# A scan layer and an attention layer in one kernel: block the scan on TensorE, move small operations to GpSimd, reorder all engines

## The chip, the cores and the metric
The kernel runs on one core of a Trainium2 chip, as one launch. The metric is the device time of that launch in microseconds (us); smaller is better. The core has TensorE (PE, matmuls; its weight loads are listed as PEld), VectorE (DVE), ScalarE (ACT), GpSimd (POOL) and SyncE (SP), which here only issues DMAs. Each engine works through its own instructions in order, and they wait for one another by semaphores.

## The reference
The input x is 128 sequences of 64 tokens of 256 channels, fp32, and cond is 128 x 512. Two layers are added to x one after the other:

```
xr, gate = split(x @ W_in.T); xr += cond; xc = silu(causal conv, 4 taps, of xr)
xn = layernorm(xc) * g + b                       # 512 channels
Bm, Cm, dt = split(xn @ W_xproj.T, 3)            # 16 states each
dt = tanh(dt @ W_dt.T + b_dt) * 0.01;  Ad = 1 + dt * (-tanh(A_log));  Bd = Bm * min(norm(xn), 1)
h = clip(h * Ad + Bd x xn, -10, 10); y_t = C_t . h       # 64 steps in order, h: 16 x 512
x = x + (y + D * xn) * silu(gate) @ W_out.T
# second layer: x * style, layernorm, q, k, v by 256 x 256 weights scaled per sequence,
# softmax attention of 16 heads over the 64 tokens, output projection, and a skip projection of v
x = x + attention(x, styles = cond)
```

## The kernel before
**Tiles and chains.** A tile is two sequences, 128 tokens: 64 tiles. The scan works on chains of 8 sequences (4 tiles): 8 sequences x 16 states fill the 128 partitions, 16 chains in all. Even chains run in lane r = 0, odd ones in lane r = 1, half a chain apart, so that both lanes are live most of the time. One step of the program advances each lane by a slice of 8 scan steps.

**Three parts.** Part A makes xn and B, C, dt of a tile; xn goes to DRAM in three bf16 parts (`a_parts`, `xn_parts`), whose sum is nearly the fp32 value, and D * xn too (`a_dx`). Part B is the scan. `prepare` turns dt of a chain into a running product `pr` and its reciprocal `rp`, so that the scan becomes an addition with clipping. On TensorE, `spread` makes the increment of one scan step in one lane: one bf16 matmul of 64 rows into `ps_u` [128, 512]. On VectorE, `scan_step` adds it to the state with bounds `hi` and `lo` (one custom instruction, L1429) into a ring `gc` of four. On TensorE, `read_out(u)` contracts two states in both lanes with the spread-out C (`cms`) into `ps_y`, 32 columns for each of four column groups. ScalarE copies `ps_y` to `y_sb`, SyncE stores it. Part C loads a tile's y (`c_y`) and D * xn (`c_dx`), adds them (`c_sum_skip`), multiplies by the silu of the gate (`c_gate_product`), projects out (`c_project_out`), adds the residual (`c_residual`, `c_x1`), and then does the attention layer.

**The order of the work** is written out by hand: each engine has a function `step(i)` with one long list of pieces, called for i = 0, 1, ... A piece's argument says how many steps behind it runs: `a_transpose_x(i)` works on tile i, `a_stats(i - 2)` on tile i - 2, scan slices on `sig = i - SCAN_LAG`, part C on `c0 = i - C_LAG` and below. There are 88 steps. Three PSUM banks (`bank[0..2]`) are passed around; `taken(...)` names the reader that must be done with a bank before the next matmul writes it. So each wait is either for data or for a buffer, and what stands ahead of a waiting piece on its engine doesn't matter, only what stands behind it.

**Pieces named below.** On SyncE: `store_parts`, `store_out`, `store_dx`, `load_wu`, `load_s1`, `load_xs` (six DMAs, 1 MB, the operand of the next slice), `store_y` (four DMAs), `load_y` (c_dx, then c_y, the latter behind the stores of the whole chain), `load_x`, `load_cx`, `store_bct`; and once per chain `load_raw`, `store_b`, `load_w` (the weights of the spread). On GpSimd: `a_half`, `a_sum` (the sum of the four taps), `a_var`, `a_root`, `a_bias`, `a_gain`, `a_shift` (xn), `a_skip`, `a_first_rest` and `a_second_rest` (the second and third bf16 part), `c_style`, `c_join`, `c_final`. On VectorE besides the scan: `a_silu`, `a_stats`, `a_mean_var`, `a_take_bc`, `a_scale_b`, `a_offset`, `spread_c`, `c_silu`, `c_max`, `c_subtract` and others. In the profile, L797 is `spread`, L813 `read_out`, L741 `a_transpose_x`, L823 `c_transpose_x`, L780 `a_transpose_bc`, L881 `c_project_k`, L1390 `a_scale_b`, L1440 `spread_c`, L1461 `c_gate_product`, L525 `a_half`, L591 `a_second_rest`, L651 `c_join`, L541 `a_var`.

## Time and profile before
| | |
|---|---|
| median of 3 runs | 2017.59 us (2012.55 to 2017.72) |
| the profiled execution | 2018.07 us, span 2016.3 us |
| mean granted TensorE clock | 0.917 of full speed |
| TensorE busy | 1736.2 us (86%), 12460 matmuls |
| TensorE weight loads | 1108.4 us (55%), beside the matmuls |
| VectorE busy | 1552.4 us (77%), 2754 instructions |
| ScalarE busy | 1161.7 us (58%) |
| GpSimd busy | 1024.1 us (51%), 1360 instructions |
| DMA moved | 224.25 MB, mean 111 GB/s |

The span runs from the first to the last instruction of the profiled execution; the execution's own time is a little longer. Busy is time in which the engine works on at least one instruction, as a sum over the span. The pipeline fills and drains, so a share of the whole span is a mean over very different stretches: TensorE is busy for half of the first tenth and for nearly all of the middle. The granted clock is in parts of full speed (1.0 is 2.4 GHz, 0.5 is 1.2 GHz). A matmul of fp32 data appears as two instructions. A row of the order of time may merge several instructions of a group; what stands in brackets is the idle time ahead of it and what ended that.

### The profile page before, as it was taken

To read this page: it belongs to the slowest core of one execution; us is meant where nothing else is said; L and a number is where in the kernel's file an instruction comes from. 1 tells how busy PE (TensorE), PEld (TensorE's weight loads), DVE (VectorE), ACT (ScalarE), POOL (GpSimd) and SP (SyncE) were. 2 spreads that over 40 slices of the span, in tenths; PEclk is the share of its full clock that TensorE was granted. 3 is DMA by queue.
4 is the path that set the end of the run, shared out by engine and by line. 5 is a ranking of instruction groups with operands and counts; after the bars stand their busy time and mean duration, and the time that the engine had idled before them with its cause. 6 is when DMAs were issued, how large, how long until landed. Compare 5 with 4: busy or idle time off the path is not lost. (4 is left out here: it accounts for less than half of the span.)

```text
span 2016.3 us, 41197 instructions
## 1 busy us (share of the span) xinstructions
PE 1736.2 (86%) x12460; PEld 1108.4 (55%) x12460; DVE 1552.4 (77%) x2754; ACT 1161.7 (58%) x2921; POOL 1024.1 (51%) x1360
## 2 busy tenths in 40 slices
PE   5337677889999999999999999999999989999775
PEld 4224333446666656666656666656665555555564
DVE  1515588889999999999999999989998888754332
ACT  4455554466676767676767676767676434344433
POOL 1576655566566656565666665656564521111220
PEclk8556788899999999999999999999999999999888
DMA  3013344555554555555554555555555554431200
GB/s 94 30 51 82 87 115 115 131 138 134 125 135 131 133 129 135 134 135 136 133 130 125 124 135 128 133 125 132 133 135 130 128 118 107 103 87 56 66 29 20
DMA packets 222713, 224.25 MB, mean 111 GB/s; under 512 B 54240, under 2 KB 179552, under 8 KB 222496
## 3 DMA queue, kind: packets, MB, share of 16 engines
q1 hardware_dynamic: 222496, 221.62, 44.3%
q8 instruction: 104, 1.70, 0.4%
q14 instruction: 113, 0.93, 0.2%
HBM read 150.36 MB, written 71.17 MB: 110 GB/s over the span
## 5 line engine op out<-in xcount | busy, mean ns | idle before, releaser
L1429 DVE CUSTOM_DVE_ANT_0 gc<-ps_u,gc,hi 128x512 f32<-128x512 f32 x1008 | 781.5, 799 | 109.8 <-PE ps_u L797 90.9
L813 PE MATMUL ps_y<-gc,cms 128*32 128x512 f32 x2048 | 309.2, 641 | 0.8 <-DVE cms L1440 0.7
L797 PE MATMUL ps_u<-xs_sb,stage 64*128 64x512 bf16 x1024 | 256.9, 467 | 28.8 <-DVE gc L1429 25.3
L1084 ACT ACTIVATE a_tap<-a_xr,conv_w 128x128 f32<-128x128 f32 x768 | 244.4, 395 | 9.4 <-DVE a_xr L1334 9.0
L797 PEld LDWEIGHTS ps_u<-xs_sb,stage 64*128 64x128 bf16 x1024 | 92.2, 167 | 282.7 <-issue 174.4
L541 POOL TENSOR_TENSOR a_ve<-a_mv,eps 128x1 f32<-128x1 f32 x64 | 12.1, 189 | 446.8 <-DVE a_mv L1361 446.8
L751 PE MATMUL ps<-a_xT,WinT 128*128 128x128 f32 x1024 | 157.9, 318 | 76.7 <-ACT a_z L1101 72.2
L751 PEld LDWEIGHTS ps<-a_xT,WinT 128*128 128x128 f32 x1024 | 145.0, 226 | 107.9 <-issue 102.5
L525 POOL TENSOR_TENSOR a_tap<-a_tap 128x512 f32<-128x512 f32 x128 | 159.7, 1269 | 58.0 <-ACT a_tap L1084 58.0
L1227 ACT ACTIVATE c_e<-c_s 128x512 f32<-128x512 f32 x128 | 80.6, 630 | 176.5 <-DVE c_s L1519 175.0
L1205 ACT ACTIVATE c_kbd<-ps,mask 128x256 f32<-128x256 f32 x256 | 100.3, 474 | 102.3 <-PE ps L881 102.3
L651 POOL TENSOR_TENSOR c_f<-c_f 128x256 f32<-128x256 f32 x64 | 46.8, 731 | 206.1 <-DVE c_f L1544 205.9
L850 PE MATMUL ps<-WoutT,c_ygT 128*128 128x256 f32 x512 | 138.1, 419 | 0.5 <-ACT c_xT L1155 0.5
L832 PE MATMUL ps<-WinT,c_xT 128*128 128x512 f32 x256 | 131.1, 635 | 0.0
L870 PE MATMUL ps<-c_zT,L1T 128*128 128x128 f32 x1024 | 125.0, 275 | 2.1 <-DVE c_sg L1452 2.1
L870 PEld LDWEIGHTS ps<-c_zT,L1T 128*128 128x128 f32 x1024 | 121.0, 192 | 3.7 <-issue 2.7
L599 POOL TENSOR_TENSOR a_nrm<-a_ss,half_pow 128x1 f32<-128x1 f32 x64 | 50.6, 791 | 140.6 <-ACT a_xg L1117 140.6
L850 PEld LDWEIGHTS ps<-WoutT,c_ygT 128*128 128x128 f32 x512 | 104.8, 216 | 15.5 <-issue 1.3
L622 POOL TENSOR_TENSOR c_xm<-c_x,c_s 128x256 f32<-128x256 f32 x64 | 47.9, 748 | 127.2 <-DVE c_x L1468 120.3
L1334 DVE TENSOR_TENSOR a_xr<-ps,condT 128x512 f32<-128x512 f32 x64 | 43.7, 682 | 82.0 <-PE ps L751 76.3
L1084 ACT ACTIVATE a_tap<-a_xr,conv_b,conv_w 128x128 f32<-128x128 f32 x256 | 105.1, 487 | 0.0
L881 PE MATMUL ps<-c_zT,L1T 128*128 128x128 f32 x512 | 84.4, 315 | 20.5 <-DVE a_bc L1382 20.5
(165 smaller groups left out, 3709.4 us busy)
## 6 DMA issues: line engine op xcount, KB each, us to landing
xs_sb<-xn_parts SPq DMA_DIRECT2D x256, 192.0 KB
xn_parts<-a_parts SPq DMA_DIRECT2D x128, 192.0 KB, 3.2
skip_d_xn<-a_dx SPq DMA_DIRECT2D x64, 256.0 KB, 8.0
xs_sb<-xn_parts SPq DMA_DIRECT2D x128, 128.0 KB
scan_out<-y_sb SPq DMA_DIRECT2D x256, 64.0 KB
c_dx<-skip_d_xn SPq DMA_DIRECT2D x64, 256.0 KB, 3.7
c_y<-scan_out SPq DMA_DIRECT2D x64, 256.0 KB, 4.8
c_wu<-style_rows SPq DMA_DIRECT2D x128, 128.0 KB, 3.0
```

The lines of the kernel that those rows point to most:

```text
L525: pool.tensor_tensor(first, first, second, ALU.add).then_inc(s[f"a_half{h}"], 1)
L751: mm = pe.matmul(ps[:, m * TOK:(m + 1) * TOK], WinT[:, k, m * P:(m + 1) * P], a_xT[:, k, :], start=(k == 0), stop=(k == KC - 1))
L797: pe.matmul(ps_u[r][t % 2][:, :], weights[:, :, l * STEPS + t], xs_sb[rows, l % 2, t, :], start=True, stop=True).then_inc(s[f"b_u{r}"], 1)
L813: pe.matmul(ps_y[quad:quad + 32, :], cms[:, v, r, 32 * u:32 * (u + 1)], gc[r][:, (2 * u + v) % RING, :], start=(u == 0), stop=(u == UNITS ...
L832: mm = pe.matmul(ps[:, :], c_xT[:, k, :], WinT[:, k, DI:2 * DI], start=(k == 0), stop=(k == KC - 1))
L850: mm = pe.matmul(ps[:, 0:DM], c_ygT[:, m, :], WoutT[:, m, :], start=(m == 0), stop=(m == MC - 1))
L870: mm = pe.matmul(ps[:, (o + c) * TOK:(o + c + 1) * TOK], L1T[:, w, k, c * P:(c + 1) * P], c_zT[:, k, :], start=(k == 0), stop=(k == KC - 1))
L881: mm = pe.matmul(ps[:, c * TOK:(c + 1) * TOK], L1T[:, 1, k, c * P:(c + 1) * P], c_zT[:, k, :], start=(k == 0), stop=(k == KC - 1))
L1084: ins = act.activation(a_tap[:, tap, m, :].rearrange("p (r t) -> p r t", r=2), a_xr[:, m, :, tap:tap + S], ACT.Identity, bias=bias, scale= ...
L1205: ins = act.activation(c_kbd[:, h, :, :].rearrange("p k t -> p (k t)"), ps[:, 0:KC * TOK], ACT.Copy, scale=mask4[:, h:h + 1])
L1227: act.activation(c_e[:, g, :], c_s[:, g, :, :].rearrange("p h t -> p (h t)"), ACT.Exp)\
L1429: dve._custom_dve(bass.dve_ops.TENSOR_ADD_SAT, out=gc[r][:, t % RING, :], in0=ps_u[r][t % 2][:, :], in1=before, s0=hi[:, c % 4, col:col + ...
```

## The change
The arithmetic stays the same except for the form of a few small operations. What changes:

1. **Scan block.** `spread(2k)`, `spread(2k + 1)` and a readout stand together on TensorE as `scan_block(sig, k)`, four times a step; the readout is that of the block before (`read_out(k - 1)`, and for k = 0 the last one of the slice before). Before, the eight spreads and four readouts stood apart among the other work.
2. **VectorE to GpSimd.** `a_offset` (as a product and a sum), `a_scale_b`, `spread_c`, `c_gate_product`, and all of the preparation of a chain but the first three operations (`split_b`, 8 operations in place of 8). `cms` gets a second buffer.
3. **New order** of the lists of all five engines, with shorter lags: `SCAN_LAG` 8 for 9, `C_LAG` 16 for 17, part C from c0 to c0 - 4 in place of c0 to c0 - 6; 84 steps in place of 88.

```diff
@@ constants
-    SCAN_LAG = 9
-    C_LAG = 17
-    STEP_COUNT = TILES + C_LAG + 7
+    SCAN_LAG = 8
+    C_LAG = 16
+    STEP_COUNT = TILES + C_LAG + 4
@@ TensorE
+            def scan_block(sig, k):
+
+                spread(sig, 2 * k)
+                spread(sig, 2 * k + 1)
+                if k > 0:
+                    read_out(sig, k - 1)
+                else:
+                    read_out(sig - 1, UNITS - 1)
@@ GpSimd, moved here from VectorE
+            def spread_c(sig):
+                for r in range(2):
+                    if chain_of(sig, r):
+                        c, l = chain_of(sig, r)
+                        pool.wait_ge(s["b_prep"], PREP * (c + 1))
+                        pool.wait_ge(s[f"b_read{r}"], 8 * (HEAD + slice_no(c, l) - 1))
+                        pool.tensor_tensor(
...
+            def c_gate_product(n):
+                if not on(n):
+                    return
+                pool.wait_ge(s["c_sg"], at(n))
+                pool.wait_ge(s["c_yd"], at(n))
+                pool.wait_ge(s["c_ygTp"], at(n - 1))
+                pool.tensor_tensor(c_yg[:, :], c_yd[:, :], c_sg[:, :], ALU.mult).then_inc(s["c_yg"], 1)
...
@@ SyncE's step
+                store_parts(i - 4)
+                store_out(c0 - 4)
+                store_dx(i - 3)
+                load_wu(c0 - 3)
+                load_s1(c0)
+                load_xs(sig + 1, 0)
+                load_xs(sig + 1, 1)
                 store_y(sig - 1)
+                load_y(c0)
                 load_x(i + 1)
+                if chain_due(i, 1) is not None:
+                    store_b(chain_due(i, 1))
+                    load_w(chain_due(i, 1))
+                load_cx(c0 + 1)
+                store_bct(i - 3)
                 if chain_due(i, 2) is not None:
                     load_raw(chain_due(i, 2))
@@ GpSimd's step, as it is now
+                if chain_due(i, 1) is not None:
+                    split_b(chain_due(i, 1))
+                spread_c(sig)
+                a_var(i - 2)
+                a_root(i - 2)
+                a_bias(i - 2)
+                a_scale_b(i - 3)
+                a_half(i - 1, 0)
                 c_sum_skip(c0)
+                c_gate_product(c0)
...
+                a_sum(i - 1)
+                a_second_rest(i - 3)
+                c_style(c0)
+                a_first_rest(i - 2)
+                c_var(c0)
+                c_root(c0)
                 a_norm_root(i - 2)
```

On TensorE, in a steady step, around the readout at the step's border; before (L797 is `spread`, L813 `read_out`; L823, L892 and L918 transpose, L850 is `c_project_out`):

```order
L813 MATMUL ps_y<-gc,cms 32x512 x4
L797 MATMUL ps_u_0<-xs_sb,stage 128x512 x2
L823 MATMUL ps<-ident,c_x 128x128 x2
L892 MATMUL ps<-ident,c_vd 128x128 x4
L797 MATMUL ps_u_1<-xs_sb,stage 128x512 x2
L918 MATMUL ps<-ident,c_e 128x128 x4
L850 MATMUL ps<-WoutT,c_ygT 128x256 x4
L918 MATMUL ps<-ident,c_e 128x128 x4
L797 MATMUL ps_u_0<-xs_sb,stage 128x512 x2
```

And after, the scan block k = 2 and the next one (L868 is `spread`, L884 `read_out`, L922 transposes yg, L989 are the scores, L931 is `c_project_out`):

```order
L868 MATMUL ps_u_0<-xs_sb,stage 128x512 x2
L868 MATMUL ps_u_1<-xs_sb,stage 128x512 x2
L884 MATMUL ps_y<-gc,cms 32x512 x4
L922 MATMUL ps<-ident,c_yg 128x128 x4
L989 MATMUL ps<-c_kbd,c_q 64x256 x8
L931 MATMUL ps<-WoutT,c_ygT 128x256 x4
L868 MATMUL ps_u_0<-xs_sb,stage 128x512 x2
L868 MATMUL ps_u_1<-xs_sb,stage 128x512 x2
L884 MATMUL ps_y<-gc,cms 32x512 x4
```

Two pairs of spreads and a readout now stand together, with three or four other pieces between two blocks.

On SyncE, from `store_bct` on, an ordinary step before:

```order
L340 DMA b_c_dt<-a_bcT 48x2x64
L455 DMA out_dram<-c_out 128x256
L411 DMA scan_out<-y_sb 8x4x512 x4
L447 DMA c_wu<-style_rows 64x512 x2
L332 DMA a_x<-in_x_dram 128x256
L351 DMA xn_parts<-a_parts 192x1x512 x2
L420 DMA c_dx<-skip_d_xn 128x512
L422 DMA c_y<-scan_out 128x512
L400 DMA xs_sb<-xn_parts 24x8x512 x2
L400 DMA xs_sb<-xn_parts 16x8x512
L400 DMA xs_sb<-xn_parts 24x8x512 x2
L400 DMA xs_sb<-xn_parts 16x8x512
```

And after, from `store_parts` on:

```order
L353 DMA xn_parts<-a_parts 192x1x512 x2
L457 DMA out_dram<-c_out 128x256
L360 DMA skip_d_xn<-a_dx 128x512
L449 DMA c_wu<-style_rows 64x512 x2
L440 DMA c_s<-style_rows 64x256 x2
L402 DMA xs_sb<-xn_parts 24x8x512 x2
L402 DMA xs_sb<-xn_parts 16x8x512
L402 DMA xs_sb<-xn_parts 24x8x512 x2
L402 DMA xs_sb<-xn_parts 16x8x512
L413 DMA scan_out<-y_sb 8x4x512 x4
L422 DMA c_dx<-skip_d_xn 128x512
L424 DMA c_y<-scan_out 128x512
```

The load of c_y stood ahead of the six loads of xs and behind one group of stores of y; it now stands behind both.

On GpSimd, from `c_sum_skip` (the row of c_yd) on, before:

```order
L614 TENSOR_TENSOR c_yd<-c_dx,c_y 128x512
L576 TENSOR_TENSOR a_xn<-a_xg,b_row 128x512
L599 TENSOR_TENSOR a_nrm<-a_ss,half_pow 128x1
L622 TENSOR_TENSOR c_xm<-c_x,c_s 128x256
L606 TENSOR_TENSOR a_dx<-a_xn,d_row 128x512
L584 TENSOR_TENSOR a_r<-a_xn,a_parts 128x512
L541 TENSOR_TENSOR a_ve<-a_mv,eps 128x1
L542 TENSOR_TENSOR a_nmu<-a_mv,neg_one 128x1
L550 TENSOR_TENSOR a_rs<-a_ve,half_pow 128x1
L558 TENSOR_TENSOR a_nb<-a_rs,a_nmu 128x1
```

And after, from the row behind `c_sum_skip`, the gate product, to `a_second_rest`:

```order
L679 TENSOR_TENSOR c_yg<-c_yd,c_sg 128x512
L716 TENSOR_TENSOR c_f<-c_f 128x256
L569 TENSOR_TENSOR a_xg<-a_z,g_row 128x512
L709 TENSOR_TENSOR c_nb<-c_rs,c_nmu 128x1
L579 TENSOR_TENSOR a_xn<-a_xg,b_row 128x512
L663 TENSOR_TENSOR a_dx<-a_xn,d_row 128x512
L528 TENSOR_TENSOR a_tap<-a_tap 128x512
L723 TENSOR_TENSOR c_out<-c_f,c_x 128x256
L611 TENSOR_TENSOR a_base<-g_proj,a_nb 128x48
L614 TENSOR_TENSOR a_base<-a_base,b_proj 128x48
L536 TENSOR_TENSOR a_cv<-a_tap 128x512
L594 TENSOR_TENSOR a_parts<-a_r,a_parts 128x512
```

The sum of c_y and c_dx was followed by operations on tiles whose gate product came a step later on VectorE; now the gate product of the same tile is the next row, and the row of a_parts comes last of the twelve.

## Rows read from the trace of the kernel before
**Rows 1.** Stretches: length, busy us of PE, PEld, DVE, ACT, POOL; clock, DMA
```profile
527.50:1516.70 989.20, 955.52 (x7335) 613.59 (x7336) 912.48 (x1620) 670.86 (x1711) 601.41 (x798) 0.98 0.53 132
1516.70:1852.60 335.90, 306.81 (x2203) 186.37 (x2203) 255.86 (x452) 144.42 (x335) 95.38 (x152) 0.95 0.44 105
1852.60:2016.00 163.40, 116.35 (x912) 94.22 (x912) 50.81 (x102) 63.60 (x148) 29.20 (x52) 0.86 0.14 43
```

**Rows 2.** TensorE on a_x (whole run, then 527 to 1517) and c_x
```profile
L741 PE MATMUL ps<-ident,a_x x128: 272/292/476, 29.3 to 1516.8; 128*128 128x128 f32 x128
L741 PE MATMUL ps<-ident,a_x x78: 272/283/303, 527.5 to 1516.8; 128*128 128x128 f32 x78
L823 PE MATMUL ps<-ident,c_x x128: 272/300/473, 332.1 to 1910.4; 128*128 128x128 f32 x128
```

**Rows 3.** TensorE in order of time, an ordinary step (start, length)
```profile
1067.01 0.30 PE L780 MATMUL ps<-ident,a_bc 128*128 128x128 f32 x1 [0.35 <-DVE c_s L1519]
1067.24 1.07 PE L813 MATMUL ps_y<-gc,cms 128*32 128x512 f32 x8
1068.24 0.47 PE L797 MATMUL ps_u<-xs_sb,stage 64*128 64x512 bf16 x2
1068.63 0.44 PE L823 MATMUL ps<-ident,c_x 128*128 128x128 f32 x2
```

**Rows 4.** The same, a step in which a chain is prepared
```profile
1023.65 2.04 PE L881 MATMUL ps<-c_zT,L1T 128*128 128x128 f32 x8 [1.96 <-DVE a_bc L1382]
...
1025.63 1.94 PE L813 MATMUL ps_y<-gc,cms 128*32 128x512 f32 x8
```

**Rows 5.** VectorE's groups by line (busy us, mean ns, idle before and releaser)
```profile
L1429 DVE CUSTOM_DVE_ANT_0 gc<-ps_u,gc,hi 128x512 f32<-128x512 f32 x1008 | 781.5, 799 | 109.8 <-PE ps_u L797 90.9 <-PE ps_y L813 0.4
...
L1440 DVE TENSOR_TENSOR cms<-cp,mask 128x64 f32<-128x64 f32 x128 | 75.9, 653 | 0.0
...
L1461 DVE TENSOR_TENSOR c_yg<-c_yd,c_sg 128x512 f32<-128x512 f32 x64 | 47.5, 742 | 0.0
```

**Rows 6.** The scaling of B on VectorE, 527 to 1517 (ns min/median/max)
```profile
L1390 DVE TENSOR_SCALAR a_bc<-a_bc,a_nrm x38: 224/1160/1171, 542.8 to 1506.8; 128x16 f32<-128x16 f32 x38
```

**Rows 7.** SyncE in order of time, an ordinary step (start, length)
```profile
1069.21 2.78 SPq L411 DMA_DIRECT2D scan_out<-y_sb  x4
1072.10 1.14 SPq L447 DMA_DIRECT2D c_wu<-style_rows  x2
1073.97 1.23 SPq L351 DMA_DIRECT2D xn_parts<-a_parts  x2
1075.29 0.56 SPq L420 DMA_DIRECT2D c_dx<-skip_d_xn  x1
1075.89 0.44 SPq L422 DMA_DIRECT2D c_y<-scan_out  x1
1076.38 2.71 SPq L400 DMA_DIRECT2D xs_sb<-xn_parts  x6
1079.13 0.68 SPq L358 DMA_DIRECT2D skip_d_xn<-a_dx  x1
1079.86 1.14 SPq L438 DMA_DIRECT2D c_s<-style_rows  x2
```

**Rows 8.** Landing of the loads of c_y, 527 to 1517
```profile
DMA to landing us min/median/max: 2.9/4.8/7.6
```

**Rows 9.** Landing of the loads of c_x, 527 to 1517
```profile
DMA to landing us min/median/max: 4.1/6.9/8.7
```

**Rows 10.** GpSimd in order of time (start, length)
```profile
1064.26 2.49 POOL L525 TENSOR_TENSOR a_tap<-a_tap 128x512 f32<-128x512 f32 x2
...
1066.70 1.15 POOL L591 TENSOR_TENSOR a_parts<-a_r,a_parts 128x512 bf16<-128x512 f32 x1
...
1087.91 0.73 POOL L651 TENSOR_TENSOR c_f<-c_f 128x256 f32<-128x256 f32 x1
```

**Rows 11.** GpSimd's longest wait, 527 to 1516 (us in total, times, longest)
```profile
POOL a_ve L541 <- DVE a_mv L1361: 303.1, 38, 12.4
```

More of the change, by code:

```diff
@@ L103, in mamba_attention_kernel @@
         eps = sb("eps", [P, 2])
+        bounds = sb("bounds", [P, 2])
         zeros = sb("zeros", [P, DI])
@@ L241, in mamba_attention_kernel @@
         head_start = {
-            "dve": """a_xr:1 a_xc:1 a_bnd:1 a_mv:1 a_nm:1 a_base:1 a_bc:1 a_bs:1 b_g0:1 b_g1:1 b_cms0:1 b_cms1:1
-                c_sg:1 c_yg:1 c_x1:1 c_st1:1 c_mv:1 c_q:1 c_vs:1 c_mx0:1 c_mx1:1 c_sub0:1 c_sub1:1 c_rc:1 c_o:1 c_f:1""",
+            "dve": """a_xr:1 a_xc:1 a_bnd:1 a_mv:1 a_nm:1 a_bc:1 b_g0:1 b_g1:1
+                c_sg:1 c_x1:1 c_st1:1 c_mv:1 c_q:1 c_vs:1 c_mx0:1 c_mx1:1 c_sub0:1 c_sub1:1 c_rc:1 c_o:1 c_f:1""",
             "pe": """a_xTp:1 a_inp:1 a_xcT:1 a_proj:1 a_bcTp:1 b_u0:8 b_u1:8 b_read0:8 b_read1:8 c_xTp:1 c_gate:1 c_ygTp:1
@@ L502, in _ @@
             pool.memset(neg_one[:, :], -1.0)
+            pool.memset(bounds[:, 0:1], CLIP)
+            pool.memset(bounds[:, 1:2], -CLIP)
             pool.memset(a_bc[:, :], 0.0).then_inc(s["w_bc"], 1)
@@ new lines, in a_scale_b, with split_b @@
+            def a_scale_b(n):
+                if not on(n):
+                    return
+                pool.wait_ge(s["a_bc"], at(n))
+                pool.wait_ge(s["a_nm"], at(n))
+                pool.tensor_tensor(a_bc[:, 0:DS], a_bc[:, 0:DS], a_nrm[:, 1:2].to_broadcast([P, DS]), ALU.mult)\
+                    .then_inc(s["a_bs"], 1)
+            def split_b(c):
+                k, done = c % 4, PREP * c
+                pool.wait_ge(s["b_pr"], 3 * (c + 1))
+                if c > 0:
+                    pool.wait_ge(s["b_bst"], 48 * c)
+                if c >= 4:
+                    pool.wait_ge(s[f"b_g{c % 2}"], HEAD + STEPS * slice_no(c - 4, SLICES))
+                pool.tensor_tensor(bd[:, :], raw[:, 0, :], rp[:, :], ALU.mult).then_inc(s["b_prep"], 1)
+                pool.tensor_tensor(b_parts[:, 0, :], raw[:, 0, :], rp[:, :], ALU.mult).then_inc(s["b_prep"], 1)
+                pool.tensor_tensor(cp[:, k, :], raw[:, 1, :], pr[:, :], ALU.mult).then_inc(s["b_prep"], 1)
+                pool.wait_ge(s["b_prep"], done + 2)
+                pool.tensor_tensor(bd[:, :], bd[:, :], b_parts[:, 0, :], ALU.subtract).then_inc(s["b_prep"], 1)
+                pool.tensor_tensor(hi[:, k, :], rp[:, :], bounds[:, 0:1].to_broadcast([P, S]), ALU.mult).then_inc(s["b_prep"], 1)
+                pool.wait_ge(s["b_prep"], done + 4)
+                pool.tensor_tensor(b_parts[:, 1, :], bd[:, :], zeros[:, 0:S], ALU.add).then_inc(s["b_prep"], 1)
+                pool.tensor_tensor(lo[:, k, :], rp[:, :], bounds[:, 1:2].to_broadcast([P, S]), ALU.mult).then_inc(s["b_prep"], 1)
+                pool.wait_ge(s["b_prep"], done + 6)
+                pool.tensor_tensor(b_parts[:, 2, :], bd[:, :], b_parts[:, 1, :], ALU.subtract).then_inc(s["b_prep"], 1)
@@ L1029, in _ @@
+                c_transpose_p(c0 - 2, 0, bank[0],
+                              taken(("c_sub0", c0 - 2), ("c_vs", c0 - 2), ("c_sg", c0), ("c_xT", c0),
+                                    ("a_bc", i - 3)))
             for i in range(STEP_COUNT):
@@ L1453, in c_silu @@
                     .then_inc(s["c_sg"], 1)
-            def c_gate_product(n):
-                if not on(n):
-                    return
-                dve.wait_ge(s["c_sg"], at(n))
-                dve.wait_ge(s["c_yd"], at(n))
-                dve.wait_ge(s["c_ygTp"], at(n - 1))
-                dve.tensor_tensor(c_yg[:, :], c_yd[:, :], c_sg[:, :], ALU.mult).then_inc(s["c_yg"], 1)
             def c_residual(n, ps):
```

331 lines of the change are left out of this document (136 added, 195 removed).

## The prediction
> **What bounds the kernel now.** I read the split of the span into stretches first, then the times at which a step begins, then the order of time on TensorE, on SyncE's queue and on GpSimd. The run has three stretches. From 527.5 to 1516.7 us all three parts work (input part A, scan, output part C) and TensorE is busy 955.5 of 989.2 us at a granted clock of 0.98, VectorE 912.5, ScalarE 670.9, GpSimd 601.4 [rows 1]. The transposition that opens a step of A runs 78 times there, two per step, so 38 steps lie between the first and the last: 989.2 / 38 = 26.0 us a step [rows 2]. Then 13 steps with scan and C in 336 us, and the rest of C in 163 us at a clock of 0.86 [rows 1].
>
> In an ordinary step TensorE waits for almost nothing: the one wait seen is 0.35 us, before the transposition of a_bc [rows 3]. In every fourth step, where VectorE prepares the coefficients of a chain, it waits 1.96 us and then runs at half speed for a while: the readout takes 1.94 where it takes 1.07 otherwise [rows 3, 4]. So the steady stretch is bound by TensorE, with VectorE (24.0 us busy a step) close behind. GpSimd is idle about 8 us a step waiting for a_mv alone (303 us in 38 waits) [rows 11].
>
> **TensorE's work.** Eight pairs of scan matmuls stand alone now, and each costs 0.39 us from its start to the next operation's start (1068.24 to 1068.63) [rows 3]. The readout, two passes of 512 columns by four column groups, costs 1.00 (1067.24 to 1068.24) [rows 3]. Half of one such fp32 pass is about 0.2, my estimate of what a bf16 pair streams; the other 0.2 is what entering and leaving costs. The change puts two pairs and a readout in one block, so four such costs go: 4 x 0.2 = 0.8, and about six fewer changes of shape altogether, 0.2 to 0.3 more. Bounds: nothing, and 4 x 0.39 = 1.6. I take 1.0. The waits of rows 3 and 4 are worth another (0.35 x 4 + 1.96 + about 2 of slow clock) / 4 = 1.3. TensorE alone would then allow 26.0 - 1.0 - 1.3 = 23.7, or nearer 23.3 with the small waits that I can't show one by one.
>
> **VectorE's work.** What leaves it: two spreads of C (75.9 us over the run, 1.2 a step), the gate product (47.5, so 0.74), the offset (some half a us, an estimate), the scaling of B, and eight of the eleven preparing operations every fourth step. The scaling of B takes 0.22 undisturbed and 1.16 at the median, although it has 16 columns: it sits behind a running GpSimd operation [rows 5, 6]. Together 3.5 to 4 us a step. VectorE would need 20 to 20.7, of which 16 scans take 12.8 (16 x 0.799) [rows 5]. In its new order the scans of one block end just as TensorE comes to the next block, so VectorE is no bound below 23.3; in a preparing step its three remaining operations (an estimated 1.2 us, by the small operations' sizes) delay TensorE by an estimated 0.7.
>
> The Trainium skill ("SBUF — State Buffer", Who interferes with whom) says that VectorE and GpSimd share one pair of ports, that the first holds it for its whole instruction and the second blocks. Rows 6 agree (0.22 against 1.16). By that rule the move gains a little more than the instructions' own length, and what the new GpSimd operations can block in return are the few VectorE operations with two SBUF operands. It changes no term below.
>
> **GpSimd's and SyncE's work, where I see the new bound.** GpSimd gets the gate product (about 1.23 us, as half of the 2.49 for two operations of the same size), two small operations for the offset, the scaling, two spreads of C, and the preparation: 601.4 / 38 = 15.8 becomes about 19.3 us a step, which would fit in 23.3 by itself. What does not fit is the order. Now the load of y (c_y) is issued a whole period before the sum that reads it, and ahead of the six loads of xs [rows 7]. In the changed kernel SyncE's step i begins with storing the three parts of tile i-4, and the third part is made by GpSimd's second_rest in step i-1, one of its last operations there. Only behind it come out, dx, wu, s1, all six xs and the four stores of y, then c_dx and c_y. And GpSimd needs that c_y in the same step i, for sum_skip, with the gate product behind it, which TensorE needs for the transposition of yg. This closes a ring: second_rest, store of parts, SyncE's queue, landing of c_y, sum_skip, GpSimd's in-order operations, next second_rest.
>
> Its length from rows. SyncE: two parts 1.32 (1073.97 to 1075.29); out about 0.5 (as c_y, 0.44, and the gap); dx 0.73; wu and s1 1.2 each (1.14 and the gap); xs 2.75; y stores 2.89; c_dx 0.60; sum 11.2 us until c_y is issued [rows 7]. Landing of c_y: 2.9 at the least, 4.8 at the median, 7.6 at most [rows 8]; the median is one in which the xs burst follows and shares the engines. Here 1 MB of xs is issued 3.5 to 6 us ahead of it and mostly done; I take 4.2. For the upper end, c_x, issued about 2 us behind the burst and its follower dx, lands in 6.9 [rows 9]. GpSimd from sum_skip to the end of second_rest: seven operations of 128x512 at 1.23 = 8.6, two of 128x256 at 0.7, c_bias 0.15 and the two small ones of the offset about 0.7 (estimates from the gaps between sizes), second_rest 1.1 [rows 10]; sum 12.0. With 0.1 for the handover the ring is 11.2 + 4.2 + 12.1 = 27.5. Where a chain has just ended (every fourth step) c_y must also wait for the landing of the y stores: last issued at about 10, landed at 13, c_y 3.2 later, 0.8 later than otherwise. Mean 27.6, against 26.0 now. TensorE has 3 to 4 us to spare in it, idles before the transposition of yg, and will run at half speed behind it as in rows 4; that costs the spare time, not the step. Ends: 26.3 with the least landing, 30.2 with that of c_x.
>
> The Trainium skill ("DMA: Bandwidth & Descriptors", Queues, rings and completion order) says that the completion signal of a transfer is a strongly ordered write, which lands only after every earlier write of the same DMA engine. That c_x takes 6.9 behind xs agrees. By it c_y cannot complete before the whole of xs and the y stores; whether that is past already when it is issued decides between my 4.2 and the second rival.
>
> **The sum**, against the execution's own 2018.07 (span 2016.3 and 1.8 around it; it lies 0.5 above the median of the three runs, 2017.59).
> Start to the first step with C: now 332.1 us for 17 steps [rows 2], 29.3 of it before the first; 17.8 a step. After: 16 steps, one less, and 1.1 less in each, since its length is then set by GpSimd's operations of A (seven at 1.23, 1.1, and about 3 of small ones, 12.7) and a chain of some 3 us through tanh, ScalarE's copies and TensorE back to a_mv, where now it is also ScalarE's taps (bounds 0 and 3): 29 + 16 x 16.7 = 296.
> To the last step of A: 47 steps, three at 25 while C fills (no out, no wu, no final operations) and 44 at 27.6: 75 + 1214 = 1289, so 1585. Now it is 1516.7: this stretch, which now takes 1184.6, becomes 104 slower and eats more than the fill gains.
> The 13 steps with scan and C: two at 27.6, two at 24 while A's operations thin out, then GpSimd's A work and store_parts are gone and the ring goes through the output instead: s1, xs, y, c_dx 7.5, landing 4.2, two operations 2.5, yg, scores and out 4.5 to 6, residual and style 1.3, so 20 to 22.5: five at 22.5, four with one chain at 20. Sum 295 (now 336).
> The rest of C: four steps at 17 and three stages of the last tile, 42: 110 (now 163; 84 steps in place of 88, and three steps of delay inside C in place of five).
> 296 + 1289 + 295 + 110 = 1990, and 1.8: about 1992, which is 1.3% less than 2018.07. The gain is wholly that of start and end (36 + 41 + 53 = 130), less 104 in the middle.
>
> **The rivals.**
> First: the ring doesn't bind, since SyncE runs ahead or its issues overlap. Then TensorE's 23.3 and the preparing steps (0.7 / 4) leave 23.7: 46 steps x 3.9 = 179 less, 1813. For it speaks that GpSimd's slack is large now; against it, that second_rest stands at the end of GpSimd's step in the order itself, and that every number in SyncE's 11.2 is a measured start to a start. Chance 0.13.
> Second, the slower side: the same ring, with c_y behind the burst. If it lands in 6.9 as c_x does, the ring is 30.2 and the time 1992 + 46 x 2.6 = 2112. It decides from the landing at which 46 x (P - 27.6) eats the 26 us of gain: P = 28.2, a landing of about 4.8 us in the plain steps, the very median of now. Issues that stretch under load do the same (c_y's own 0.44 is short only where nothing blocks it). Chance 0.30 in all, most of it between 2025 and 2090.
> Third: the merging gives TensorE nothing. Under the ring that is not seen at all; only in the first case would it cost 46 x 1.0.
> Fourth: gains and losses nearly cancel, by small waits in start and end: 2012 to 2024. Chance 0.07.
>
> **How the numbers follow.** The forecast, ring at 26.3 to 28.0, has 0.50; its own range is 1930 to 2012. A measurement of this kernel tells 0.3% from no change, so 2012 to 2024 counts as the same. Faster: 0.50 and 0.13, less the forecast's upper edge 0.02, 0.61. Same: 0.09. Slower: 0.30. The range leaves out the first rival's fast core and the top of the second: 1890 to 2085.
>
> **What would show it.** In the profile after: GpSimd idle before c_yd, released by the DMA of c_y, 3 to 5 us in nearly every steady step; TensorE idle before the transposition of c_yg, with the clock falling behind it; a_x transpositions 27.6 apart; c_y landing 3 to 5 us after an issue about 11 us behind the first store of parts. VectorE's busy time a step near 20 and TensorE's idle time several us show the first two parts right even if the time is not. I am wrong if c_y is issued much less than 11 us behind the first store of parts, if GpSimd finds c_y landed and waits elsewhere, or if steps come 24 us apart.

## The result, and the profile after

The changed kernel takes 2237.1 us (median of 4 runs, 2231.7 to 2242.8) against 2015.6 us before, measured beside it: 11% slower, ratio 1.109, 95% interval 1.106 to 1.113. The forecast was 1992 us, range 1890 to 2085. The profiled execution has a span of 2230.0 us.

By stretch, after (columns as in [rows 1]): the three parts together, scan and output, the rest of the output.

```profile
527.50:1767.00 1239.50, 1004.51 (x7621) 651.39 (x7618) 815.10 (x1409) 699.40 (x1779) 750.42 (x1140) 0.89 0.47 109
1767.00:2072.00 305.00, 263.00 (x1987) 158.33 (x1987) 208.44 (x354) 130.07 (x306) 114.19 (x198) 0.96 0.44 106
2072.00:2230.00 158.00, 112.88 (x768) 82.80 (x767) 43.77 (x88) 52.30 (x121) 31.94 (x52) 0.78 0.13 39
```

TensorE was busy 97% of the steady stretch before and is busy 81% of it now, with the granted clock down from 0.98 to 0.89. Its operations that mark the steps (answer to [rows 2]):

```profile
L812 PE MATMUL ps<-ident,a_x x128: 272/292/476, 28.8 to 1767.2; 128*128 128x128 f32 x128
L904 PE MATMUL ps<-ident,c_x x128: 272/273/447, 308.0 to 2153.8; 128*128 128x128 f32 x128
```

The first output step comes at 308, 24 us earlier than before. The last step of A starts at 1767, where it stood at 1516.7: that is 250 us later. From there to the end it is 463 us, where it was 499. So the whole loss, and more, is in the steps that carry A, whose period is 31.3 us on the mean in place of 26.0.

Where they wait is in three groups by line (columns as in [rows 5]):

```profile
L671 POOL TENSOR_TENSOR c_yd<-c_dx,c_y 128x512 f32<-128x512 f32 x64 | 80.8, 1262 | 402.9 <-DMA c_dx<-skip_d_xn 284.8
L1532 DVE TENSOR_REDUCE c_mx<-ps 128x8 f32<-128x512 f32 x128 | 82.5, 686 | 343.0 <-PE ps L989 343.0
L922 PE MATMUL ps<-ident,c_yg 128*128 128x128 f32 x256 | 65.1, 403 | 282.1 <-POOL c_yg L679 282.1
```

They are one chain. VectorE waits for TensorE's scores, TensorE waits for GpSimd's gate product, and GpSimd waits for the loads of c_dx and c_y. One step of it in order of time, SyncE first (answer to [rows 7]), with the four loads and stores between 948.5 and 952.3 left out:

```profile
947.25 1.24 SPq L353 DMA_DIRECT2D xn_parts<-a_parts  x2
...
952.29 2.74 SPq L402 DMA_DIRECT2D xs_sb<-xn_parts  x6
955.08 2.79 SPq L413 DMA_DIRECT2D scan_out<-y_sb  x4
957.97 0.39 SPq L422 DMA_DIRECT2D c_dx<-skip_d_xn  x1
958.40 0.42 SPq L424 DMA_DIRECT2D c_y<-scan_out  x1
...
977.83 1.25 SPq L353 DMA_DIRECT2D xn_parts<-a_parts  x2
```

GpSimd in the same step, from one second rest (L594) to the next:

```profile
946.01 1.16 POOL L594 TENSOR_TENSOR a_parts<-a_r,a_parts 128x512 bf16<-128x512 f32 x1
...
965.59 1.26 POOL L671 TENSOR_TENSOR c_yd<-c_dx,c_y 128x512 f32<-128x512 f32 x1 [5.48 <-DMA c_dx<-skip_d_xn]
966.99 1.26 POOL L679 TENSOR_TENSOR c_yg<-c_yd,c_sg 128x512 f32<-128x512 f32 x1
...
976.57 1.18 POOL L594 TENSOR_TENSOR a_parts<-a_r,a_parts 128x512 bf16<-128x512 f32 x1
```

TensorE (answer to [rows 3, 4]):

```profile
956.47 0.68 PE L868 MATMUL ps_u<-xs_sb,stage 64*128 64x512 bf16 x4
957.08 1.07 PE L884 MATMUL ps_y<-gc,cms 128*32 128x512 f32 x8
...
968.30 1.12 PE L922 MATMUL ps<-ident,c_yg 128*128 128x128 f32 x4 [4.73 <-POOL c_yg L679]
969.35 1.99 PE L989 MATMUL ps<-c_kbd,c_q 64*64 64x256 f32 x16
```

The ring closes without a gap. The second rest ends at 947.17 and SyncE stores the parts 0.08 later. c_y is issued at 958.40, 11.15 behind the parts, and the sum starts at 965.59, 7.19 behind the issue. The next second rest ends at 977.75, 12.16 behind the sum's start, and SyncE stores the next parts 0.08 later. This step is 30.6 us. Over steps 20 to 63 the four pieces are, on the mean, 0.1, 11.8, 7.2 and 12.1, together 31.2, in three of four steps. In the fourth, where a chain has just ended and c_y waits for the landing of its stores, they are 0.1, 16.6, 2.8 and 12.1, together 31.7. The measured mean is 31.3. The profile names c_dx as what ended GpSimd's wait, but it is c_y that does: in the trace c_y lands 0.12 us before the sum starts for each of the 64 tiles, and c_dx at least 0.6 us before it. Behind its 4.73 us of waiting TensorE runs at the lower clock level (granted 0.51 from 968 to 974): the scores (L989) take 1.99 here and 1.09 in a step without the wait.

Landing of the loads of c_y over the steady steps, 527 to 1400 (min/median/max; answer to [rows 8], 2.9/4.8/7.6):

```profile
DMA to landing us min/median/max: 2.6/6.9/8.7
```

The 2.6 are the steps behind a chain's end, where c_y is issued 5 us later, once the stores of y have landed; there it lands as fast as it does ahead of the burst in the experiments below.

### The profile page after: what moved, and what is told of

Read it like the earlier page. It is cut to its first block and busy times, and to the rows that moved or that the text cites. A ratio compares the mean times of both kernels' runs of the same rounds, so it can differ in the third digit from the quotient of the medians.

```text
span 2230.0 us, 41407 instructions
## 1 busy us (share of the span) xinstructions
PE 1744.8 (78%) x12460; PEld 1109.5 (50%) x12460; DVE 1349.0 (60%) x2306; ACT 1163.6 (52%) x2921; POOL 1222.4 (55%) x1874
## 2 busy tenths in 40 slices
DMA packets 222715, 224.27 MB, mean 101 GB/s; under 512 B 54240, under 2 KB 179552, under 8 KB 222496
## 5 line engine op out<-in xcount | busy, mean ns | idle before, releaser
L884 PE MATMUL ps_y<-gc,cms 128*32 128x512 f32 x2048 | 306.1, 628 | 6.5 <-POOL cms L650 6.5
L671 POOL TENSOR_TENSOR c_yd<-c_dx,c_y 128x512 f32<-128x512 f32 x64 | 80.8, 1262 | 402.9 <-DMA c_dx<-skip_d_xn 284.8
L1532 DVE TENSOR_REDUCE c_mx<-ps 128x8 f32<-128x512 f32 x128 | 82.5, 686 | 343.0 <-PE ps L989 343.0
L922 PE MATMUL ps<-ident,c_yg 128*128 128x128 f32 x256 | 65.1, 403 | 282.1 <-POOL c_yg L679 282.1
L1240 ACT ACTIVATE c_ygT<-ps 128x512 f32<-128x512 f32 x64 | 38.2, 597 | 409.0 <-PE ps L922 409.0
L868 PE MATMUL ps_u<-xs_sb,stage 64*128 64x512 bf16 x1024 | 196.1, 432 | 20.0 <-issue 12.0
L922 PEld LDWEIGHTS ps<-ident,c_yg 128*128 128x128 f32 x256 | 41.9, 200 | 337.8 <-POOL c_yg L679 333.6
L931 PE MATMUL ps<-WoutT,c_ygT 128*128 128x256 f32 x512 | 169.8, 488 | 1.6 <-ACT c_ygT L1240 1.6
L931 PEld LDWEIGHTS ps<-WoutT,c_ygT 128*128 128x128 f32 x512 | 122.6, 253 | 64.9 <-issue 38.2
L822 PEld LDWEIGHTS ps<-a_xT,WinT 128*128 128x128 f32 x1024 | 135.4, 213 | 23.2 <-issue 18.9
L951 PE MATMUL ps<-c_zT,L1T 128*128 128x128 f32 x1024 | 125.0, 275 | 1.1 <-DVE c_sg L1481 1.1
L694 POOL TENSOR_TENSOR c_ve<-c_mv,eps 128x1 f32<-128x1 f32 x64 | 12.1, 190 | 202.1 <-DVE c_mv L1505 202.1
L868 PEld LDWEIGHTS ps_u<-xs_sb,stage 64*128 64x128 bf16 x1024 | 72.9, 187 | 90.3 <-issue 64.1
L989 PE MATMUL ps<-c_kbd,c_q 64*64 64x256 f32 x1024 | 113.7, 585 | 3.9 <-DVE c_vsT L1513 3.9
L544 POOL TENSOR_TENSOR a_ve<-a_mv,eps 128x1 f32<-128x1 f32 x64 | 12.1, 190 | 185.3 <-DVE a_mv L1431 184.4
```

The costliest lines, as they stand in the source:

```text
L822: mm = pe.matmul(ps[:, m * TOK:(m + 1) * TOK], WinT[:, k, m * P:(m + 1) * P], a_xT[:, k, :], start=(k == 0), stop=(k == KC - 1))
L868: pe.matmul(ps_u[r][t % 2][:, :], weights[:, :, l * STEPS + t], xs_sb[rows, l % 2, t, :], start=True, stop=True).then_inc(s[f"b_u{r}"], 1)
L884: pe.matmul(ps_y[quad:quad + 32, :], cms[:, slice_no(*chain_of(sig, r)) % 2, v, r, 32 * u:32 * (u + 1)], gc[r][:, (2 * u + v) % RING, :], ...
L922: mm = pe.transpose(ps[:, m * TOK:(m + 1) * TOK], c_yg[:, m * P:(m + 1) * P], ident[:, :])
L931: mm = pe.matmul(ps[:, 0:DM], c_ygT[:, m, :], WoutT[:, m, :], start=(m == 0), stop=(m == MC - 1))
L951: mm = pe.matmul(ps[:, (o + c) * TOK:(o + c + 1) * TOK], L1T[:, w, k, c * P:(c + 1) * P], c_zT[:, k, :], start=(k == 0), stop=(k == KC - 1))
```

## The experiments

The theory: the period is the ring, and what makes it 31.3 and not 27.6 is that c_y lands behind the burst of xs. The rivals: the late landing costs by itself whoever waits; or the added GpSimd work or TensorE's new order is what is slow. All times below are medians, and the ratios are against the kernel before, run on the same chip in the same job (2014.3 to 2017.8 us).

**c_y ahead of xs.**
```diff
                 load_s1(c0)
+                store_y(sig - 1)
+                load_y(c0)
                 load_xs(sig + 1, 0)
                 load_xs(sig + 1, 1)
-                store_y(sig - 1)
-                load_y(c0)
```


> The changed kernel with one edit in SyncE's order: store_y and load_y stand ahead of the six loads of xs instead of behind them. Theory (the ring second_rest, store of parts, SyncE's queue, landing of c_y, GpSimd's 12.15 us back to second_rest): c_y is issued 2.75 us earlier, 8.9 us behind the first store of parts, and lands in about 4.8 us as in the kernel before, where it also stood ahead of the burst, not in 7.2. The ring is 8.9 + 4.8 + 12.15 = 25.9 us in place of 31.2, over 47 steps 250 us less: about 1985 us. Rival (GpSimd's added work, or TensorE's slow clock, sets the period and the wait for c_y is only where its spare time shows): the wait moves elsewhere and the time stays within 20 us of 2237.

Measured: 1953.6 us, ratio 0.969 (0.964 to 0.975). The move of two lines takes 283 us from the changed kernel. c_y now lands in

```profile
DMA to landing us min/median/max: 2.8/3.3/5.8
```

and is issued 8.5 us behind the second rest at the median, so the ring is 24 (8.5, 3.3 and 12.2) and TensorE is 95% busy. The landing is 1.5 us shorter than I had expected, and the time is 31 us below the expected 1985. Most plain steps take 24 to 25 us. Every fourth one, where a chain starts, takes 26 to 31: there SyncE stores B behind the xs loads and waits 6.2 us for that store to land before it can load W (`stage`). The steps' mean is 25.6.

```profile
999.47 1.49 SPq L375 DMA_DIRECT2D b_parts<-b_parts_sb  x3
1007.14 4.73 SPq L387 DMA_DIRECT2D stage<-b_parts  x8
```

**c_y first of all**, the same two lines at the head of SyncE's step, ahead of the parts.


> The changed kernel with store_y and load_y at the head of SyncE's step, ahead of store_parts. Theory: c_y no longer depends on second_rest of the step before; it hangs on ScalarE's copy of the readout alone and is issued some 6 us after the step's begin on TensorE. The ring is gone, and the period is the larger of TensorE's 23.3 us and VectorE's, with the preparing steps some 24 us: 47 x 7.2 = 340 us less, about 1895 us. Rival (the ring is only one of several of nearly this length, or GpSimd's order sets about 26 us by itself): 1980 us or more.

Measured: 2103.4 us, ratio 1.044 (1.036 to 1.051): missed by 200 us, although c_y landed in 3.0 us at the median. Waits over 600 to 1600 us (total, times, longest):

```profile
DVE c_f L1565 <- DMA c_wu<-style_rows: 95.2, 32, 4.1
...
PE ps L851 <- DVE c_f L1565: 65.0, 31, 3.4
```

I had thought of one ring and made another. The load of wu waits for c_f of the tile before and now stood 3.9 us later in SyncE's step, and VectorE's next c_f waits for it with TensorE behind. The repair, wu ahead of y:
```diff
+                load_wu(c0 - 3)
                 store_y(sig - 1)
                 load_y(c0)
                 store_parts(i - 4)
                 store_out(c0 - 4)
                 store_dx(i - 3)
-                load_wu(c0 - 3)
```


> SyncE's step of the changed kernel in the order wu, y stores, c_dx, c_y, x parts, out, dx, s1, xs and the rest: as the version with y first (2103.4 us, where VectorE waited 76.9 us for c_wu), but the load of wu is at the head. Theory (that version's loss came from wu standing behind the x parts, a second ring): the waits for c_wu go, the steps fall from 28.2 to about 25 us, total about 1930 to 1960. Rival (the loss is the W load of the chain-start steps and the x parts themselves coming late): 2080 to 2110, no change.

Measured: 1979.3 us, ratio 0.981 (0.975 to 0.988), 124 us less. The theory's cause holds and its size was 20 us too hopeful: the plain steps are 23.2 us now, TensorE's own, but the chain starts 28.5 to 33.

**The parts stored later**, behind the load of s1: out, dx and wu are issued before the second rest is done, but s1 still waits for c_xm, which GpSimd makes right behind it, and c_y stays behind xs.
```diff
-                store_parts(i - 4)
                 store_out(c0 - 4)
                 store_dx(i - 3)
                 load_wu(c0 - 3)
                 load_s1(c0)
+                store_parts(i - 4)
```


> The changed kernel with store_parts behind load_s1 instead of at the head of SyncE's step. Theory: the ring does not open, since load_s1 waits for c_xm, which GpSimd makes right behind second_rest; but the store of out, that of dx and the load of wu then run ahead of the waiting. From the end of second_rest to the issue of c_y: 0.7 (c_style) + 1.27 + 1.29 + 2.75 + 2.85 + 0.6 = 9.5 us in place of 11.7. Period 29.1 with the same landing, about 2135 us. A theory in which only the third part's store gates the ring would give a large gain here (25 us a step or less, under 1960 us); one in which SyncE's queue doesn't matter, 2237 us.

Measured: 2137.4 us, ratio 1.061 (1.054 to 1.068), in steps of 29.4, as worked out from the ring. The sum agrees better than its pieces: in the plain steps c_y is issued 10.5 us behind the second rest (9.5 expected, 11.9 in the changed kernel), and it lands in 6.5 in place of 7.2. Over all the steady steps the landing is 6.4 at the median.

**Half of xs.** Each of the six xs loads moves 256 of its 512 channels and the others are zero, so this kernel computes the scan on half of its input. The packets and issues are as many as before (222715 packets in both profiles), the bytes of xs half (190.7 MB moved in all for 224.3).
```diff
-                    sp.dma_start(xs_sb[first:first + k * SEQS, l % 2, :, :],
-                                 xs_dram[c, l * STEPS:(l + 1) * STEPS, 0:k].rearrange("t q k c -> (q k) t c"))\
+                    sp.dma_start(xs_sb[first:first + k * SEQS, l % 2, :, 0:DI // 2],
+                                 xs_dram[c, l * STEPS:(l + 1) * STEPS, 0:k, :, 0:DI // 2].rearrange("t q k c -> (q k) t c"))\
...
+            dve.memset(xs_sb[:, :, :, DI // 2:DI], 0.0)
```


> The changed kernel, where the six loads of xs bring only the first 256 of the 512 channels (half a MB a step in place of one, with as many DMAs; the scan reads zeros for the others). It tells whether c_y's 7.2 us of landing are the backlog of that burst. If they are and the time goes by bytes: landing 4.5 to 5, period 28.8, about 2125 us. If the time goes by packets (as many, of 512 in place of 1024 bytes): landing 7 and 2237 us. If the landing has nothing to do with the burst (a fixed cost behind the stores of y): also 2237 us.

Measured: 2025.3 us, ratio 1.006 (1.002 to 1.009), 100 us below what I expected. c_y lands in

```profile
DMA to landing us min/median/max: 2.7/3.1/4.7
```

The steps are 27.5 us, as the pieces of the ring add up in the plain ones (11.7, 3.3 and 12.2). So what held c_y was the bytes of xs still under way 6 us behind their first issue, not its place in SyncE's list by itself.

**The second rest ahead of the sum**, on GpSimd alone; SyncE keeps the changed kernel's order.
```diff
                 a_half(i - 1, 0)
+                a_second_rest(i - 3)
                 c_sum_skip(c0)
```


> The changed kernel with one line moved on GpSimd alone: the second rest of step i-3 stands ahead of the sum with the skip instead of 10 operations behind it; SyncE's order is that of the changed kernel, c_y still behind the xs loads. Theory (the ring is x parts on SyncE, xs, landing of c_y, sum, second rest: the move takes the second rest out of it and the 31.2 us step falls; what is left is the way from the readout of y over SyncE's stores and the landing to TensorE's transposition, which allows about 24 to 26 us): about 1950 to 2000. Rival (c_y's late landing costs by itself, whatever stands behind it on GpSimd): 2237, no change, or 1.2 us a step more.

Measured: 1980.6 us, ratio 0.981 (0.977 to 0.984), with c_y still landing late:

```profile
DMA to landing us min/median/max: 2.6/6.1/8.7
```

This and the next one separate the theory from the rival. One instruction moved past the others is worth 256 us, and the landing is 6.1.

**The control: late c_y in the kernel before.**
```diff
-                load_y(c0)
                 load_xs(sig + 1, 0)
                 load_xs(sig + 1, 1)
+                load_y(c0)
```


> The kernel before the change with c_dx and c_y loaded behind the two xs loads, as the changed kernel has it, nothing else. Theory (the place behind xs costs only where a ring goes through it: here the x parts are stored two steps after the second rest that makes them, so a landing of c_y some 3 to 6 us later falls into GpSimd's idle time of 8 us a step before the variance): 2010 to 2030. Rival (a late c_y costs in any kernel, since GpSimd's step starts with it and all its work follows): 50 steps by 3 to 4 us, 2160 to 2220.

Measured: 2011.5 us, ratio 0.998 (0.996 to 1.001). Its landing and the first of its waits from 527 to 1517 us:

```profile
DMA to landing us min/median/max: 6.3/7.8/9.4
```

```profile
POOL a_ve L541 <- DVE a_mv L1361: 297.7, 38, 12.1
```

c_y lands 3 us later than in the kernel before and no engine waits for it: GpSimd's idle time before a_ve is where it was [rows 11]. Here a later landing cost nothing, since no ring of this kernel's length goes through it.

**The chain-start steps.** With y ahead of xs as in the first experiment, B's store moved ahead of y, and W between c_y and xs:


> The changed kernel with SyncE's step in the order x parts, out, dx, wu, s1, store of B (chain steps), y stores, c_dx, c_y, weights W (chain steps), xs, then the rest. With y ahead of xs alone (1953.6) the plain steps took 24.0 us and each chain-start step 27.4 to 30.6: there the store of B landed only 6.1 us after its issue, behind the xs loads, and W landed 6.2 us after that, while TensorE waited 2.4 to 3.6 us for it. Theory (the burst of xs is what makes W late as well): B's store lands in 2 to 3 us, W is there before the first increment, the 11 or so chain-start steps fall to about 24.5, total 1953 - 11 x 4.5 = about 1905. Rival (the chain-start steps are long because of their extra preparation work on VectorE and GpSimd): no change, 1950 to 1960. Rival (W's 8 issues of 4.7 us now delay xs): 1950 or more, with TensorE waiting for xs instead.

Measured: 1965.7 us, ratio 0.974 (0.969 to 0.979): a miss, not told apart from the 1953.6 us (0.964 to 0.975) of its base. B's store waits for GpSimd's split of B at the head of its step (issued at 1010.73, where SyncE was free at 1008.3), and what now waits is c_y behind it:

```profile
1018.67 1.26 POOL L672 TENSOR_TENSOR c_yd<-c_dx,c_y 128x512 f32<-128x512 f32 x1 [4.70 <-DMA c_dx<-skip_d_xn]
```

So B's store goes between the two, behind y and ahead of xs:
```diff
                 load_y(c0)
+                if chain_due(i, 1) is not None:
+                    store_b(chain_due(i, 1))
                 load_xs(sig + 1, 0)
                 load_xs(sig + 1, 1)
+                if chain_due(i, 1) is not None:
+                    load_w(chain_due(i, 1))
                 load_x(i + 1)
-                if chain_due(i, 1) is not None:
-                    store_b(chain_due(i, 1))
-                    load_w(chain_due(i, 1))
```
(with y ahead of xs as in the first experiment)


> The changed kernel with SyncE's step x parts, out, dx, wu, s1, y stores, c_dx, c_y, store of B, xs, weights W, a_x and the rest. In the version with y ahead of xs the chain-start steps took 27.4 to 30.6 us because B's store stood behind xs; in the one with B ahead of y they stayed at 29 because B waits for GpSimd's split and held back y (c_yd waited 4.7 us). Theory (neither now: B's store is issued right behind c_y and lands ahead of the xs burst): chain-start steps about 25, plain 24, total about 1905 to 1920. Rival (the chain-start steps need their 27 to 30 us for GpSimd's split at the head of the step, 2.9 us, and VectorE's preparation): 1950 to 1965.

Measured: 1897.5 us, ratio 0.939 (0.936 to 0.943), a little below what was expected. Steps of 24.6 on the mean.

**Both together**: wu, y, parts, out, dx, B, xs, W, s1, and the rest as in the changed kernel.


> SyncE's step in the order wu, y stores, c_dx, c_y, x parts, out, dx, store of B, xs, W, s1, a_x and the rest. With wu and y first (1979.3 us) the plain steps were TensorE's own 23.2 us and the chain-start steps 28.5 to 33. Theory (W is late there as elsewhere since B's store stands behind xs): chain-start steps about 26, the plain ones stay at 23.2, total about 1890 to 1910. Rival (chain-start steps bound by GpSimd's split): 1960 to 1980. What could spoil it: s1 behind xs and W comes 5 us later and holds up the style on GpSimd.

Measured: 1849.3 us, ratio 0.915 (0.912 to 0.919). It is 41 us below the lower end of what I had expected, and beats the kernel before by 8.5% and the changed one by 17%, with the same arithmetic. Stretch of the three parts:

```profile
527.00:1412.00 885.00, 875.82 (x7238) 576.12 (x7239) 765.83 (x1341) 664.97 (x1690) 714.25 (x1085) 1.00 0.64 145
```

TensorE is busy 99% at full clock, in steps of 23.2 us. With the chain starts, most of them at 24 and one at 28, the mean is 23.6. The lists of the other four engines are the changed kernel's; SyncE's list alone differs. So neither GpSimd's added work nor TensorE's new order was what made the changed kernel slow.

**The block of the scan**, first in the version with y ahead of xs, then in the fastest:
```diff
                 spread(sig, 2 * k)
-                spread(sig, 2 * k + 1)
                 if k > 0:
                     read_out(sig, k - 1)
                 else:
                     read_out(sig - 1, UNITS - 1)
+                spread(sig, 2 * k + 1)
```


> y ahead of xs (1953.6 us) with the block of the scan taken apart: the second pair of increments stands behind the readout, so that 64-row and 128-row work alternate twice as often, as before the change. TensorE is 94 to 98% busy in the steps of that kernel. Theory (the pairing itself saves TensorE time; by the busy time of the increments, 256.9 against 196.1 us in the two traces, about 1.0 us a step): slower by 1.0 us in some 60 steps, about 2010. Rival (merging gives nothing, the increments' records only look shorter): 1950 to 1960. Rival (the second increment comes later for VectorE and the wait grows): over 2040.

Measured: 1971.3 us, ratio 0.979 (0.974 to 0.984) against 0.969 (0.964 to 0.975): not told apart from its base, and about 40 us below the expected 2010. The steps that carry A are as long in both (25.5 and 25.6 on the mean), and GpSimd waits for c_y in both by about 1 us a step. That c_y's arrival hid the difference is read from these waits.

> The fastest version so far (wu and y first, xs behind B's store, s1 behind W: 1849.3 us, TensorE 99% busy at full clock in steps of 23.2 us) with each block of the scan taken apart: the second pair of increments behind the readout. Theory (a pair of its own costs 0.39 us from start to start, the two pairs of a block 0.61 together, so 0.17 us for each of four blocks are saved by the pairing): 0.7 us a step in some 44 steps and a like amount in the 12 steps of scan and C, 1880 to 1890. Prediction's own term (1.0 us a step with changes of shape at full price): 1895 to 1905. Rival (merging gives nothing): 1849, within 5.

Measured: 1888.2 us, ratio 0.939 (0.936 to 0.942) against 0.915 (0.912 to 0.919), 39 us slower, in steps of 23.9 for 23.2. Its block, and behind it that of the fastest:

```profile
840.22 0.46 PE L869 MATMUL ps_u<-xs_sb,stage 64*128 64x512 bf16 x2
840.61 1.06 PE L885 MATMUL ps_y<-gc,cms 128*32 128x512 f32 x8
841.61 0.46 PE L869 MATMUL ps_u<-xs_sb,stage 64*128 64x512 bf16 x2
842.00 1.13 PE L1035 MATMUL ps<-L1T,c_oT 128*128 128x256 f32 x4
```

```profile
830.89 0.68 PE L869 MATMUL ps_u<-xs_sb,stage 64*128 64x512 bf16 x4
831.51 1.06 PE L885 MATMUL ps_y<-gc,cms 128*32 128x512 f32 x8
832.50 1.13 PE L1035 MATMUL ps<-L1T,c_oT 128*128 128x256 f32 x4
```

From the block's start to L1035 it is 1.78 apart and 1.61 together: 0.17 each, 0.7 a step.

**The gate product back on VectorE**, `c_gate_product` behind `c_scale_v` on VectorE, first with y ahead of xs, then in the fastest version.


> y ahead of xs (1953.6 us) with the gate product c_yg back on VectorE, behind the two scalings, where the before kernel had it on VectorE as well: 1.28 us less on GpSimd, about 0.7 us more on VectorE a step. Theory (TensorE sets the plain steps and both vector engines have 3 to 4 us of slack): 1945 to 1960, no difference. Rival (GpSimd is the second bound, since c_yd to the second rest is still 12 us of a ring with the chain starts): faster by 0.5 to 1 us a step, about 1900 to 1925. Rival (VectorE, 20 us of 24, is the tighter one): slower by 0.7 us a step, about 1995.

Measured: 1933.0 us, ratio 0.958 (0.952 to 0.963), 21 us faster than its base (0.969, 0.964 to 0.975), where no difference was expected. The intervals only just miss each other. GpSimd's way from the sum to the second rest falls from 12.2 to 11.3 us, and its wait for c_y from 1.2 to 0.5 on the mean.

> The fastest version so far (1849.3 us) with the gate product back on VectorE, as in the pair 1953.6 and 1933.0 where that gave 21 us because chain-start steps and late landings ran over GpSimd. Theory (TensorE alone sets all steps here, GpSimd is busy 18.8 of 23.2 us and waits): 1845 to 1855, no difference. Rival (the steps of chain starts, 24 to 28 us, are GpSimd's): 1835 to 1843. Rival (VectorE's 0.7 us more come just before c_max): 1870 or more.

Measured: 1880.2 us, ratio 0.933 (0.930 to 0.935), 31 us slower than its base, where again no difference was expected, in steps of 23.9. The product did not cost VectorE the 0.7 us that I had counted, but 1.25 at the median (the kernel before: 673/676/1270 ns):

```profile
L1482 DVE TENSOR_TENSOR c_yg<-c_yd,c_sg x34: 826/1246/1608, 605.1 to 1399.9; 128x512 f32<-128x512 f32 x34
```

It starts while GpSimd's a_xg (L570, also 128x512) is running, and it ends 0.54 to 0.56 us behind that one: it took 0.83, 1.25 and 1.61 us where a_xg still had 0.29, 0.70 and 1.06 to go.

TensorE's weight loads wait longer for c_yg in it (first row; the second is the fastest version, both 600 to 1400 us):

```profile
PEld ps L914 <- DVE c_yg L1482: 37.7, 33, 1.6
```

```profile
PEld ps L923 <- POOL c_yg L680: 21.0, 25, 0.8
```

So the same move gained in the version in which the chain of c_y, sum and what stands behind it on GpSimd still sets steps, and lost in the one in which TensorE does. The sign of the second is shown; that these waits (17 of the 24 us that the 34 steps lost) are all of its cause is not.

## Why the prediction was wrong, point by point

**The mis-sized term is the landing of c_y.** The prediction put it at 4.2 us, "mostly done", with 6.9 as the upper end; measured it is 7.2 from the issue to the sum's start in the plain steps. The other pieces nearly stood: SyncE 11.2 forecast and 11.8 measured, GpSimd from sum to second rest 12.0 and 12.1. The plain steps came out at 31.2 in place of 27.5, of which the landing is 3.0. In the fourth steps the mis-sized landing is that of the stores of y, behind the same burst: the forecast had them landed at 13 us and the sum started at 16.2, measured c_y is issued at 16.6 and the sum starts at 19.4. The stores' own landing is some 6 us in place of 3, an estimate from their last issue at about 10.3. So the period is 31.3 in place of 27.6. The half load of xs (7.2 to about 3.1) and the load ahead of xs (3.3) show that the cause is the burst. The row that should have been taken was in hand: c_x, 2 us behind the same burst, lands in 6.9 [rows 9], while c_y's 4.8 [rows 8] is of loads issued ahead of it. I corrected the nearer row the wrong way.

The Trainium skill ("DMA: Bandwidth & Descriptors", Queues, rings and completion order) was cited for a completion that waits for every earlier write of the same DMA engine. By that rule c_y's completion waits for all of xs; the measured 7.2 behind xs and 3.1 behind half of it agree, but they agree as well with plain sharing of the engines by bytes, and no run here tells the two apart.

**The ring itself** was right, with its place and each of its stations; what it said the profile would show is there, GpSimd's wait before c_yd (6.6 us on the mean, where 3 to 5 were forecast), TensorE's before c_yg, and the lower clock behind. The second rival is what came true, beyond its own 2112: its landing of 6.9 gave 30.2, and 1.1 us more a step over 46 is 51 us, which makes 2163; the rest of the way to 2237 is mostly in the start and the end, below. It had 0.30 where it should have had most of the chance.

**The sum, by its parts**, against the profiled execution's 2230.0 + 1.8. Start to the first C step: 296 forecast, 308.0 measured, 12 over. To the last step of A: 1289 and 1459, 170 over. From there: 405 and 463, 58 over. Of these 58, 17 are in the first four steps, in which the ring still sets 28 to 31 us. 7 are in the nine steps with scan and C, which nearly all take 22.1 whether one chain or two are running (20 and 22.5 forecast), in the changed kernel and in the fastest version alike. TensorE is busy for 20.2 of the 22.1. And 33 are in what follows without scan, where a step takes 20.6 to 22.9 for the 17 forecast (17.9 to 20.3 in the kernel before). What I left out is that with little else to do the attention of one tile is a serial chain (after, a step without scan; idle in brackets):

```profile
2101.01 0.63 PE L973 MATMUL ps<-ident,c_vd 128*128 128x128 f32 x4 [0.78 <-DVE c_s L1540]
2102.96 1.25 PE L999 MATMUL ps<-ident,c_e 128*128 128x128 f32 x8 [1.32 <-ACT c_vbd L1286]
2105.48 0.66 PE L940 MATMUL ps<-ident,c_z 128*128 128x128 f32 x2 [1.27 <-ACT c_pT L1305]
2106.70 2.05 PE L962 MATMUL ps<-c_zT,L1T 128*128 128x128 f32 x8 [0.56 <-ACT c_zT L1257]
```

There are six such waits in a step without scan, 0.5 to 1.3 us each, and half speed behind the last of these (L962 takes 1.06 in a full step). With the scan two of them are left, 1.3 before L999 and 0.6 before L962. This is read from the trace; no run changed it.

**TensorE alone**: forecast 23.3 to 23.7, measured 23.2 plain and 23.6 with chain starts, in the fastest version. The pairing was taken at 1.0 us a step and is worth 0.7: 0.17 for each of four blocks where 0.2 was taken (0.8). No run takes apart the 0.2 to 0.3 for other changes of shape. The third rival, that merging gives nothing, is out.

**VectorE and GpSimd**: forecast 20 to 20.7 and 19.3 us a step, measured 815.1 and 750.4 in 39.6 steps, 20.6 and 18.9. The scaling of B takes 0.215 to 0.218 on GpSimd, where it took 1.16 at the median on VectorE [rows 6].

**The first rival**, the ring does not bind, 1813: it did bind, but the version in which it does not takes 1849. What it lies above 1813 is in the start and the end: 308 us to the first C step (296 forecast) and 438 from the last step of A (405).

## What to carry to other kernels

When a change takes steps of delay out of a pipeline, look for rings: go from the last store of one step along each in-order queue to the load that the next step's work waits for, and add up the issues, the landing and everything queued in front on each engine. Price a landing by a row with the same traffic ahead of it, not by the same load at another place. A queue's list is as much a schedule as an engine's: small loads and stores that someone waits for go ahead of the large burst, and every one moved forward pushes back the others, so ask of each what ring it is in.
